# A fused attention and FFN kernel on one core: TensorE's order inside a head, and ScalarE's and VectorE's with it

## The reference, cut to what matters

```python
B, S, D, H, HD, I = 16, 256, 512, 16, 128, 2048
n = layernorm(x)
q = (n @ Wq) / sqrt(HD);  k = ctx_2048 @ Wk;  v = ctx_2048 @ Wv      # per head of 128
attn = softmax(q @ k.T)                                             # 256 x 256 per head and batch
x = x + (attn @ v) @ Wo
y = q_act(layernorm(x))                                             # MX quantised, blocks of 32
inter = silu(y @ q_w(w_gate).T) * (y @ q_w(w_up).T)
out = x + q_act(inter) @ q_w(w_down).T
```

## Time and profile before

| | us |
|---|---|
| median of 3 runs | 2305.63 |
| range of the 3 runs | 2303.83 to 2306.59 |
| the profiled execution | 2300.67 |
| its span, first to last instruction | 2299.1 |
| PE (TensorE matmul) busy | 2098.5 (91%) |
| DVE (VectorE) busy | 1524.5 (66%) |
| ACT (ScalarE) busy | 995.3 (43%) |
| POOL (GpSimd) busy | 795.8 (35%) |
| mean granted TensorE clock, as a share of 2.4 GHz | 0.988 |

### The profile page before, as it was taken

One profiled execution on the slowest core, in us unless ns is written; L12 is line 12 of the kernel. 1 busy time (PEld: TensorE's weight loads), 2 busy tenths in 40 slices (PEclk: granted clock), 3 DMA queues, 4 the chain that ended last, 5 costly groups with the idle time before them and its releaser, 6 DMA issues.

```text
span 2299.1 us, 49730 instructions
## 1 busy us (share of the span) xinstructions
PE 2098.5 (91%) x15818; PEld 1521.5 (66%) x15818; DVE 1524.5 (66%) x3455; ACT 995.3 (43%) x2760; POOL 795.8 (35%) x1093
## 2 busy tenths in 40 slices
PE   6799999999999998989998989899999988999996
PEld 5577777777777776767776777677777873344442
DVE  6566666666666666666666666666666547777774
ACT  7654444444444444444444434444544432233332
POOL 4332332233323332332323232322121004776674
PEclk9899999999999999999999999999999999999998
DMA  6533333323332323232323232323232343454544
GB/s 222 141 90 67 72 72 71 64 67 73 72 72 67 71 63 77 63 82 56 84 54 77 61 84 61 79 61 76 47 78 52 61 111 92 83 86 81 86 80 68
DMA packets 398607, 179.55 MB, mean 78 GB/s; under 512 B 361984, under 2 KB 374784, under 8 KB 398400
## 3 DMA queue, kind: packets, MB, share of 16 engines
q1 hardware_dynamic: 375616, 125.10, 26.2%
q0 software_dynamic: 16608, 45.36, 8.0%
q10 hardware_dynamic: 6176, 6.29, 0.9%
HBM read 61.08 MB, written 27.26 MB: 38 GB/s over the span
## 4 chain that ended last, share of the span: by engine, by line
DVE 39%; PE 21%; ACT 16%; issue 12%; DMA 5%; POOL 3%; SPq 1%; DVEq 1%; ACTq 1%; POOLq 0%
ACT psplit L596 7%; DVE psplit L865 7%; PE b_qk L1013 7%; ACT prob L588 6%; DVE nmax L855 6%; PE b_v L1013 5%; DVE rsum L859 3%; DMA probT<-psplit 3%; DVE vbuf L705 3%; DVE cbuf L705 2%; DMA attn_weights<-x_scratch 2%; DVE qk L705 2%; PE b_c L1013 2%; PE b_s L1013 2%; PE b_w L1070 2%
## 5 line engine op out<-in xcount | busy, mean ns | idle before, releaser
L588 ACT ACTIVATE prob<-b_s,nmax 128x256 f32<-128x256 f32 x514 | 239.2, 470 | 756.3 <-DVE nmax L855 756.2
L865 DVE SCALAR_TENSOR_TENSOR psplit<-prob,rrec,psplit 128x256 f16<-128x256 f32 x514 | 252.5, 532 | 266.4 <-ACT psplit L596 266.4
L1013 PE MATMUL b_v<-attn_weights,kvT 128*128 128x256 f16 x3072 | 381.0, 274 | 0.7 <-POOL attn_weights L390 0.7
L1013 PE MATMUL b_qk<-xT,attn_weights 128*128 (+1 forms) x3072 | 380.1, 274 | 0.0
L1013 PE MATMUL b_qk<-kvT,attn_weights 128*128 (+1 forms) x3072 | 379.2, 273 | 0.0
L1013 PEld LDWEIGHTS b_v<-attn_weights,kvT 128*128 (+1 forms) x3072 | 302.2, 98 | 38.0 <-POOL attn_weights L390 1.3
L1013 PEld LDWEIGHTS b_qk<-xT,attn_weights 128*128 128x128 f16 x3072 | 301.9, 98 | 36.0
L1013 PEld LDWEIGHTS b_qk<-kvT,attn_weights 128*128 128x128 f16 x3072 | 301.8, 98 | 36.0
L1013 PE MATMUL b_s<-qk 128*128 128x256 f16 x1542 | 212.1, 274 | 116.9 <-DVE qk L705 99.2
L596 ACT ACTIVATE psplit<-prob,rrec 128x256 f16<-128x256 f32 x514 | 233.4, 501 | 174.1 <-DVE rrec L862 173.6
L1013 PEld LDWEIGHTS b_s<-qk 128*128 128x128 f16 x1542 | 139.8, 98 | 221.3 <-DVE qk L705 157.7
(11 more groups left out here) (124 smaller groups left out, 2790.9 us busy)
## 6 DMA issues: line engine op xcount, KB each, us to landing
ffn_w<-wffn SPq DMA_DIRECT2D x48, 256.0 KB, 3.3
acc<-xtok POOLq DMA_DIRECT2D x16, 512.0 KB, 4.0
out<-acc POOLq DMA_DIRECT2D x16, 512.0 KB, 3.6
out<-attn_weights POOLq DMA_DIRECT2D x32, 256.0 KB, 4.1
xrow<-xq POOLq DMA_DIRECT2D x61, 128.0 KB, 3.9
kvrow<-kvt POOLq DMA_DIRECT2D x61, 128.0 KB, 3.5
stage<-wattn SPq DMA_DIRECT2D x12, 512.0 KB, 3.5
ffn_scratch<-ffn_t SPq DMA_DIRECT2D x48, 128.0 KB, 1.8
```

Of the source, the lines that this page charges most:

```text
L588: last = eng.activation(half(prob, q, 256), half(bS, q, 256), ACT.Exp, bias=nmax[:, q:q + 1], scale=1.0, accum_out=rsum[:, q:q + 1])
L865: last = eng.scalar_tensor_tensor(out=p_part(k, z, 1), in0=half(prob, z, 256), scalar=rrec[:, z:z + 1], in1=p_part(k, z, 0), op0=ALU.mult, ...
L1013: last = eng.matmul(out, l, r, start=(a == 0), stop=(a == len(pairs) - 1))
```

## The change

TensorE's slot becomes Q and K, scores, V, projection, context. The wait for `qk_lo` moves from the scores to Q and K (bank `b_qk` must have been read), that for `v_lo` from the context to V, and that for `c_lo` from the context to the projection. ScalarE writes q and k hi first, and waits for `s_done` with it (which covers both the bank and the buffer `qk`); `v` hi comes between the exponential and p hi; p hi signals for each half. VectorE's order follows: `nmax`, q and k lo, one piece of the preparation, `rsum` and `rrec`, v lo, p lo (each half waits for its own p hi), context lo, the rest. `x_stats`, `kv_lo` and `x_lo` move ahead of `rsum` (`x_lo` from k = 2 to k = 3), ScalarE's `kv_prep` from k = 1 to k = 0. The function `ffn_y` is cut in two; its second part, `ffn_magic`, runs at k = 2 ahead of `rsum`.

```diff
@@ ScalarE, quad @@
                     i = 4 * n + k
+                    if front:
+                        hi(half(qk, 0), bQK[:, :], QK_OUT, "s_done", i + 1, "qk_hi")
                     if front or k == 0:
                         eng.wait_ge(sm["max_done"], i + 1)
...
-
+                    if front:
+                        hi(half(vbuf, 2 * k, 256), bV[:, 0:256], V_OUT, "v_done", i + 1, "v_hi")
+                    if front or k == 0:
                         if not isinstance(n, int) or i >= 2:
                             eng.wait_ge(sm["pt_loaded"], 16 * (i - 1))
                         eng.wait_ge(sm["rec_done"], i + 1)
                         for q in range(2):
-                            last = eng.activation(p_part(k, q, 0), half(prob, q, 256), ACT.Copy, scale=rrec[:, q:q + 1])
-                        last.then_inc(sm["p_hi"], 1)
-                    if front:
-                        hi(half(qk, 0), bQK[:, :], QK_OUT, "qk_done", i + 1, "qk_hi")
+                            eng.activation(p_part(k, q, 0), half(prob, q, 256), ACT.Copy, scale=rrec[:, q:q + 1]
+                                           ).then_inc(sm["p_hi"], 1)
                     if front or k < 2:
                         hi(half(cbuf, 2 * ((k + 2) % 4), 256), bC[:, 0:256], C_OUT, "c_done", i + 1, "c_hi")
-                    if front:
-                        hi(half(vbuf, 2 * k, 256), bV[:, 0:256], V_OUT, "v_done", i + 1, "v_hi")
-                    if prepare and k == 1:
+                    if prepare and k == 0:
                         kv_prep(n)
@@ VectorE, quad @@
+                    if front:
+                        lo(half(qk, 1), bQK[:, :], half(qk, 0), QK_OUT, "qk_hi", i + 1, "qk_lo")
+                    if prepare and k == 0:
+                        x_stats(n)
+                    if prepare and k == 1:
+                        kv_lo(n)
+                    if ffn and k == 2:
+                        ffn_magic(w)
+                    if prepare and k == 3:
+                        x_lo(n)
                     if front or k == 0:
                         eng.wait_ge(sm["exp_done"], i + 1)
...
-                        eng.wait_ge(sm["p_hi"], i + 1)
+                    if front:
+                        lo(half(vbuf, 2 * k + 1, 256), bV[:, 0:256], half(vbuf, 2 * k, 256), V_OUT,
+                           "v_hi", i + 1, "v_lo")
+                    if front or k == 0:
                         for z in range(2):
+                            eng.wait_ge(sm["p_hi"], 2 * i + z + 1)
                             last = eng.scalar_tensor_tensor(
...
-                    if front:
-                        lo(half(qk, 1), bQK[:, :], half(qk, 0), QK_OUT, "qk_hi", i + 1, "qk_lo")
@@ TensorE, scores, context and quad @@
             def scores(i):
-                eng.wait_ge(sm["qk_lo"], i)
                 eng.wait_ge(sm["exp_done"], i)
...
-                    scores(i)
-
                     if fresh:
                         wait_split(eng, n, QK_AT[k])
+                    eng.wait_ge(sm["qk_lo"], i)
                     for which, src in ((0, xb), (1, kb)):
...
-                    last.then_inc(sm["qk_done"], 1)
-
-                    context(i, k)
-
+
+                    scores(i)
+
+                    eng.wait_ge(sm["v_lo"], i)
...
                     else:
+                        eng.wait_ge(sm["c_lo"], i)
                         project(n, k, batch, place, fresh)
+
+                    context(i, k)
```

More of the change, by code:

```diff
@@ L180, in build @@
             s_done max_done exp_done sum_scaled rec_done
-            qk_done qk_hi qk_lo c_done c_hi c_lo v_done v_hi v_lo p_hi p_lo pt_loaded o_done o_added
+            qk_hi qk_lo c_done c_hi c_lo v_done v_hi v_lo p_hi p_lo pt_loaded o_done o_added
             acc_loaded x1_stored
@@ L760, in ffn_y, with ffn_magic @@
                 eng.tensor_tensor(by_block(wy[:, :]), by_block(wsrc[:, :]), spread(wi), ALU.mult).then_inc(sm["ffn_y"], 1)
+            def ffn_magic(w):
                 eng.wait_ge(sm["ffn_y"], w + 1)
@@ L873, in quad @@
                         lo(half(cbuf, at + 1, 256), bC[:, 0:256], half(cbuf, at, 256), C_OUT, "c_hi", i + 1, "c_lo")
[L874 to L878, removed]
                     if ffn and k == 0:
@@ L882, in quad @@
                         x_apply(n)
-                        kv_lo(n)
                     if ffn and k == 1:
                         ffn_y(w)
-                    if prepare and k == 2:
-                        x_lo(n)
                     if isinstance(n, int) and n == NQ and k == 0:
@@ L1051, in context @@
                 eng.wait_ge(sm["c_lo"], i)
-                eng.wait_ge(sm["v_lo"], min(i, 4 * NQ) if isinstance(i, int) else i)
                 pair, hh = (1 if k < 2 else 0), k % 2
@@ L1083, in quad_at @@
                     i = 4 * n + k
-                    scores(i)
                     if fresh:
                         wait_split(eng, n, QK_AT[k])
+                    eng.wait_ge(sm["qk_lo"], i)
                     for which, src in ((0, xb), (1, kb)):
-                        last = product(half(bQK, which, 256).rearrange("p (t f) -> p t f", t=2), [
+                        product(half(bQK, which, 256).rearrange("p (t f) -> p t f", t=2), [
                             (attn_w(n, a, QK_AT[k] * PIECE + (which * KC + c) * P, P), src[:, :, c, b, :])
                             for c in range(KC) for a, b in PARTS])
-                    last.then_inc(sm["qk_done"], 1)
-                    context(i, k)
+                    scores(i)
+                    eng.wait_ge(sm["v_lo"], i)
                     if fresh and k % 2 == 0:
@@ L1144, in _ @@
             for n in range(FFN_TO + 1, NQ):
-                if n < NQ - 4:
+                if n <= NQ - 4:
                     ready(n)
@@ L1161, in _ @@
             i = 4 * NQ
+            eng.wait_ge(sm["qk_lo"], i)
             scores(i)
-            context(i, 0)
+            eng.wait_ge(sm["c_lo"], i)
             project(NQ, 0, B - 1, 0)
             project(NQ, 1, B - 1, 0)
+            eng.wait_ge(sm["v_lo"], i)
+            context(i, 0)
             eng.wait_ge(sm["gate_up_resident"], 16)
```

## The result

| | before | after |
|---|---|---|
| median (lowest to highest, 4 runs each) | 2304.73 us (2300.59 to 2306.59) | 2191.84 us (2190.88 to 2193.51) |
| ratio, 95% interval | 1 | 0.9513 (0.9497 to 0.953) |
| profiled execution: time, span | 2300.67, 2299.1 us | 2190.88, 2189.3 us |

The change takes 112.9 us off, where 128.5 were forecast (2191.84 us for 2177). The time lies in the range (2152 to 2232) and in the likeliest case's own (2160 to 2200).

The account below looks back on a forecast made before the run. In quads 4 to 51 TensorE waited on the softmax round trip, chiefly VectorE's q and k lo. Terms of -114, -1, -12, -3 and +1.5 sum to -128.5 us, taking 2305.6 to 2177 us; range 2152 to 2232.

Parts of the forecast that it names:

- likeliest case: Whole kernel: the main forecast of 2177 us, with its own range of 2160 to 2200 and chance 0.60.
- TensorE would become the bound of quads 4 to 51: Quads 4 to 51: q and k lo gets 1.7 us spare instead of 1.0, TensorE's waits on it go; -114 us.
- The context at the slot's end costs about nothing.: Slot's end: the context's wait for the transpose of p costs at most some tenths of a us in few slots.
- I leave the 14.3 us of issue, which no order removes.: Quads 4 to 51: TensorE's ten issue waits at its loop turns stay at 14.3 us.
- more gain: Rival: the 14.3 us of issue are hidden or the first quads reach TensorE's pace; 2155 us, chance 0.13.
- GpSimd, 6 us taken, 0 and 66 as bounds: Slots k = 2: GpSimd's rounding beside `rsum` and p lo costs 6 us over 47 quads, bounds 0 and 66.
- Under 1.00 in quads 4 to 51: Sign of being wrong: TensorE's granted clock falls below 1.00 in quads 4 to 51.
- no lower one: TensorE's granted clock: with fewer waits none lower than before, and no gain beyond the one in the terms.
- other signs: Signs of being wrong: `b_c` or `b_qk` waits over 0.5 us a quad, or row maximum later than 2 us behind scores.
- Quads 0 to 3: First quads: shorter waits for GpSimd's split and the transpose behind it; -12 us, bounds -22 and +3.
- The tail: FFN: first tile's transpose stands in the SP queue behind one waiting for a later `c_done`; +1.5 us (0 to +4).
- Quad 63: Context waits behind the 4 MB load, but the transpose is wanted 2.6 us later in its slot; -3 us (0 to -6).

Follow-up runs that it names:

- e3: Kernel before with TensorE's order untouched; only ScalarE's hi of q and k moved ahead of p hi, VectorE's lo ahead of p lo: 2229.79 us, ratio 0.9676.
- e5: Changed kernel with TensorE's and VectorE's hardware loops both written out in full: 2157.47 us, ratio 0.9365.
- e8: Changed kernel with the context product right behind the scores instead of at the slot's end: 2403.22 us, ratio 1.0443.
- E7: Kernel before with the changed TensorE order alone; ScalarE and VectorE keep the split of q and k behind p: 2607.01 us, ratio 1.1318.
- e1: Changed kernel with TensorE's hardware loop alone written out in full: 2172.31 us, ratio 0.9422.
- e9: Changed kernel, loops kept; the context of a turn's last slot is issued first in the next turn, behind the branch: 2179.03 us, ratio 0.946.
- e6: e5 with the 4 MB load cut into four of 1 MB across quad 63 and the 2 MB load behind the last head's work: 2141.09 us, ratio 0.9297.
- e4: Changed kernel with VectorE's and ScalarE's preparation instructions back in their old places: 2193.68 us, ratio 0.952.
- e10: Changed kernel with VectorE's hardware loop alone written out; TensorE keeps its own: 2189.44 us, ratio 0.9511.

## Why the prediction was right, and where its sizes were off

- **TensorE would become the bound of quads 4 to 51, since lo of q and k no longer stands behind p lo.** Right. The chain, the waits and the 1.7 us spare agree, and e3 shows that this one move in VectorE's and ScalarE's lists gives two thirds. E5 shows the rest: without turns the stretch is TensorE's own 1289.6 us, against 1291 worked out.
- **"The context at the slot's end costs about nothing."** Right, and it is more than that: it is what gives the transpose its time. `b_c` waits 0.5 us in quads 4 to 62, e3 with the context in mid-slot 35.2, e8 with it behind the scores 153.4. The prediction didn't price what the old place would have cost. E7 shows that TensorE's new order without the new split is harmful (+13.2%), so neither part is the change by itself.
- **"I leave the 14.3 us of issue, which no order removes."** This step failed, in size: 36.3 us. The order does decide it. What counts is the work queued on TensorE when the branch of some 3.6 us is reached, and the new order put the branch behind the context's wait for a transpose. E1 and e5 removed it, and e9 moved it and brought the gap back to 1.49 us. Of the 36.3 us, 25.4 are the pauses themselves, 9.4 slowed products of Q and K and 1.5 the slots behind them. The rival "more gain" had it the wrong way round: it let the context at the slot's end hide the fetch.
- **GpSimd, 6 us taken, 0 and 66 as bounds.** It was 0. In quads 4 to 51 `rsum` took 0.25 us at most: GpSimd's first rounding instruction starts as it ends. P lo did stretch at k = 2, a half of it to 1.49 us from 0.49, and both to 2.12 from 0.88 in quad 40. It ended 5.36 us behind the scores (E + 5.8 was feared), its transpose landed at E + 8.6, and the context took it at E + 9.6: the transpose's spare held it, and e5 has its slots at TensorE's pace. That the term came out at nothing, and the work 1.7 us under 1291, is luck for the total: without them the gain would have missed by 22, not by 14.5, in quads 4 to 51. By the rule of the Trainium skill (GPSIMD Engine Reference, section 1, Specifications: GpSimd's interfaces to SBUF are shared with VectorE) the trace agrees in kind, in quad 2 above all, where `rsum` took 1.88 us beside GpSimd's 2.13, but not with a cost of 66.
- **Clock.** "Under 1.00 in quads 4 to 51" was named as a sign of being wrong, and 0.99 is what the window shows. It belongs to the turns: in e5 it is 1.00. So "no lower one" failed, by those 9.4 us and part of the 1.5. Of the other signs, `b_qk` came to its bound (23.8 us over 48 quads are 0.50 a quad), and the row maximum started at most 1.2 us behind the scores' start in quads 4 to 62, within the 2 allowed.
- **Quads 0 to 3**, -14.2 for -12: the mechanism as said (V's waits of 2.0 us for L390, k = 2 at 10.4 to 10.5 for 11). **Quads 52 to 62**: -0.9 for -1.
- **The tail**, +7.1 for +1.5 with +4 as bound: the step looked at SP's queue alone. The transpose of the last head but one went behind ScalarE's load of 2 MB, as it waits for a context that now stands at the slot's end. E6 issues the load later and the tail is 397.3 us, below the 398.9 of before. **Quad 63** -2.2 for -3; e6 shows 9.2 us more to be had there.
- **Preparation in new places**: costed at nothing beside the order of the split, and e4 agrees.

Open: why six of the ten turns have slow products and four don't (a gap of 2.15 us is followed by them, one of 2.56 isn't; in e4 it is five turns of ten, in e10 four, and not the same ones), and why quads 0 to 3 and quad 63 differ by some us between kernels with the same code there (quad 63: 29.1 to 32.7 in the changed kernel, e1, e4, e5, e9 and e10). No run settles either.

## What to carry to other kernels

Order an engine's list by who waits for each item and how soon: what the next slot's first product needs goes ahead of what only a DMA with spare time needs, and the consumer of that DMA goes to the slot's end. Before counting a loop turn as a constant, look what work is queued when its branch is reached: a wait that stands just ahead of the branch makes it bare. And a bulk load should not be issued between a small transfer that is waited for and its source; cut it and hang it on later work.

## What the runs showed of the hardware

- TensorE's branch of a loop took 3.6 us in the median (83 ns when it fell through), in each of before, after and e9; the next product started 4.1 to 4.2 us behind the branch's start (410.4 to 414.63, 374.5 to 378.70, 372.7 to 376.82). VectorE's branch row is 55 to 78 ns in e1, yet its next instruction started 3.4 to 3.8 us behind it (379.88 to 383.37 in the first), and a second gap of 1.3 to 1.9 us followed behind the next but one; so it was all nine times that the branch was taken.
- Gaps of 2.15 to 2.56 us were followed in six of ten cases by a granted clock of 0.50 for some us, though TensorE had been busy up to the gap; behind the ten gaps of at most 1.6 us in e9, and the ten of 1.1 to 1.8 us in the kernel before, it stayed at 1.00.
- A transpose DMA that lands in 3.0 us landed in 8.9 behind a load of 2 MB on another engine's queue, while four loads of 1 MB, spread over the heads, left TensorE without idle time in quad 63 (e6).
